# Last layer of a conditioned sequence model: where ScalarE's copies of matmul products stand in its order

## The reference

```python
h, gate = _adaln(x, c, adaln_mamba_w, adaln_mamba_b)
h_fwd = _ssm(h, fwd_in_w, fwd_xproj_w, ...)
h_bwd = jnp.flip(_ssm(jnp.flip(h, 1), bwd_in_w, ...), 1)
x = x + gate * (h_fwd + h_bwd)
h, gate = _adaln(x, c, adaln_mlp_w, adaln_mlp_b)
return x + gate * (jax.nn.silu(h @ mlp_w1) * (h @ mlp_w2) @ mlp_w3)

def _ssm(h, in_w, xproj_w, dt_bias, A_log, Dskip, out_w):
    xs, z = jnp.split(h @ in_w, 2, axis=-1)
    xs = jax.nn.silu(xs)
    proj = xs @ xproj_w                       # 512 dt, 64 B, 64 C
    dt = jax.nn.softplus(proj[..., :512] + dt_bias)
    # scan over tokens, 512 channels x 64 states:
    # hst = hst * exp(dt * A) + (dt * x) * B ;  y = sum over states of hst * C
    return (y + xs * Dskip) * jax.nn.silu(z) @ out_w
```

## Time and profile before

| | us |
|---|---|
| median of 3 runs (4523.04 to 4531.2) | 4526.49 |
| the profiled execution | 4523.65 |
| its span, first to last instruction | 4521.8 |

### The profile page before, as it was taken

How to read it: one execution, slowest core, us unless ns; L and a number is a source line. 1 busy time by engine, 2 the same in 40 slices (tenths; PEclk the granted TensorE clock), 3 DMA queues, 4 the chain that set the end, 5 groups by cost and what they waited for, 6 DMA issues and landing times.

```text
span 4521.8 us, 80784 instructions
## 1 busy us (share of the span) xinstructions
PE 4262.2 (94%) x31308; PEld 3470.6 (77%) x31308; DVE 4061.9 (90%) x3951; ACT 3941.5 (87%) x6178; POOL 3810.0 (84%) x1522
## 2 busy tenths in 40 slices
PE   8989899899899998999999999999999999999998
PEld 5448788778778774458888888888888888888887
DVE  5659999999899986649999999999999999999996
ACT  4559999899899974559999999999999999999995
POOL 3329999899889883339999999999998999999996
PEclk8999999999999999999999999999999999999999
DMA  4001221111111221022242322322322422323221
GB/s 165 1 15 68 57 64 64 56 59 64 57 57 65 63 82 40 1 45 71 73 86 75 91 65 79 80 74 80 82 76 69 83 80 90 64 80 64 76 81 39
DMA packets 241388, 303.31 MB, mean 67 GB/s; under 512 B 116448, under 2 KB 175712, under 8 KB 241008
## 3 DMA queue, kind: packets, MB, share of 16 engines
q1 hardware_dynamic: 241008, 298.15, 23.5%
HBM read 289.84 MB, written 8.26 MB: 66 GB/s over the span
## 4 chain that ended last, share of the span: by engine, by line
PE 41%; ACT 39%; DVE 12%; issue 5%; POOL 3%; DVEq 0%; DMA 0%; SPq 0%; POOLq 0%; ACTq 0%
PE psum L1109 11%; ACT weights_c L1684 10%; PE psum L1093 10%; PE psum L834 8%; ACT work L1705 8%; ACT work L1684 7%; ACT weights_c L1705 6%; DVE work L2155 6%; PE psum L1209 5%; DVE weights_c L2155 3%; PE psum L1090 2%; ACT L1416 2%; ACT modulation L1684 2%; POOL work L2573 1%; PE psum L1290 1%
## 5 line engine op out<-in xcount | busy, mean ns | idle before, releaser
L2573 POOL TENSOR_TENSOR work<-work,weights_a 128x2048 f32<-128x2048 f32 x512 | 1979.0, 3876 | 57.7 <-DVE work L2155 56.9
L2155 DVE TENSOR_TENSOR_SCAN work<-weights_c,psum 128x512 f32<-128x512 f32 x1316 | 1506.6, 1203 | 61.9 <-PE psum L1093 42.4
L1109 PE MATMUL psum<-ident,work 128*128 128x128 f32 x8192 | 1237.3, 274 | 12.1 <-POOL work L2573 11.8
L2573 POOL TENSOR_TENSOR weights_c<-weights_c,weights_a 128x2048 f32<-128x2048 f32 x256 | 990.4, 3877 | 14.2 <-DVE weights_c L2155 13.0
L1093 PE MATMUL psum<-ident,work 128*128 128x128 f32 x5464 | 952.5, 277 | 45.4 <-DVE weights_c L2155 13.3
L1109 PEld LDWEIGHTS psum<-ident,work 128*128 128x128 f32 x8192 | 968.0, 142 | 18.7 <-POOL work L2573 18.1
L1684 ACT ACTIVATE work<-work,decay 128x504 f32<-128x504 f32 x1172 | 819.0, 709 | 44.5 <-DVE weights_c L2155 24.1
L1093 PEld LDWEIGHTS psum<-ident,work 128*128 128x128 f32 x5464 | 658.9, 142 | 237.2 <-issue 129.3
L1093 PE MATMUL psum<-ident,weights_c 128*128 128x128 f32 x4432 | 784.9, 278 | 50.2 <-DVE work L2155 30.3
L2155 DVE TENSOR_TENSOR_SCAN work<-work,psum 128x512 f32<-128x512 f32 x586 | 675.9, 1202 | 24.0 <-PE psum L1093 17.0
L2155 DVE TENSOR_TENSOR_SCAN weights_c<-work,psum 128x512 f32<-128x512 f32 x586 | 677.5, 1203 | 20.9 <-PE psum L1093 18.5
(11 more groups left out here) (221 smaller groups left out, 6216.7 us busy)
## 6 DMA issues: line engine op xcount, KB each, us to landing
weights_a<-c_rows SPq DMA_DIRECT2D x384, 512.0 KB, 3.7
work<-b_diagonals SPq DMA_DIRECT2D x240, 128.0 KB, 2.4
weights_c<-b_diagonals SPq DMA_DIRECT2D x112, 128.0 KB, 2.4
b_diagonals<-weights_c SPq DMA_DIRECT2D x1, 4096.0 KB, 19.5
weights_c<-in_L_cond_fwd_in_w SPq DMA_DIRECT2D x8, 512.0 KB, 5.3
weights_c<-in_L_cond_fwd_xproj_w SPq DMA_DIRECT2D x4, 1024.0 KB, 7.1
weights_c<-in_L_cond_bwd_in_w SPq DMA_DIRECT2D x8, 512.0 KB, 5.2
weights_c<-in_L_cond_bwd_xproj_w SPq DMA_DIRECT2D x4, 1024.0 KB, 7.0
```

The lines of the kernel that those rows point to most:

```text
L1109: last = nc.tensor.matmul(PS[:, i, k * P:(k + 1) * P], flat[:, at:at + P], IDENT[:, :], start=begins and k == 0, stop=ends and k == DC - 1 ...
L2155: v.tensor_tensor_scan(buf["ring"][s % RING][:, along, j], buf["decay"][q % DECAYS[l]][:, along], PS[:, 4 + q % LOOKAHEAD, along], 0.0, AL ...
L2573: g.tensor_tensor(state, state, row.unsqueeze(2).broadcast_to([P, T, DC]), ALU.mult).then_inc(ss["prod_ready"], 1)
```

## The change

Five numbers in ScalarE's generator change, all of them the `later` of a copy in the last layer. For z the outer wait goes from 1 to 0 and the inner one from 2 to 0, for in and gate the inner one from 2 to 0: these copies stand two steps sooner, right behind ScalarE's own work of the step in which TensorE has the last piece. bt, dtx0 and dtx1 stand two steps sooner as well, and bc four steps sooner, two steps ahead of the one with its last piece. The copies of dt, the silu and softplus blocks, layer 1 and what is prepared before run 0 keep their places. Nothing is added or taken away, and the rows of TensorE, VectorE, GpSimd and SyncE are the same.

```diff
@@ scaled_inputs, of both state space layers
-                        yield plan.read(f"dtx{t}", 0 if l == 1 and r % 2 else 2)
+                        yield plan.read(f"dtx{t}", 0 if l == 3 or r % 2 else 2)
@@ beside3, of the last layer
                     def copy(name, dst):
-                        yield plan.read(name, 2)
+                        yield plan.read(name, 0)
...
                     def gates(*chunks):
                         for j in chunks:
-                            yield plan.read(f"z{j}", 1)
+                            yield plan.read(f"z{j}", 0)
...
-                        yield plan.read("bc", 2)
+                        yield plan.read("bc", -2)
...
-                        yield plan.read("bt", 2)
+                        yield plan.read("bt", 0)
```

## The result

| | us |
|---|---|
| median before, the 8 executions taken beside the changed kernel | 4526.9 (4522.63 to 4531.24) |
| median after, 8 executions | 4539.73 (4534.73 to 4541.15) |
| ratio, with its 95% interval | 1.0026 (1.0017 to 1.0035) |
| span of the profiled execution, before and after | 4521.8, 4537.0 |

What follows compares the result with a forecast made beforehand. No engine alone bounds the kernel; VectorE's scan chain is closest, with 82 us idle. Cost 11.2 us behind the silu blocks less 6.7 gained gave +4.5, 4531 us; forecast 4526 to 4535.5 (chance 0.60), range 4520 to 4542.

Steps and rivals of the forecast that it cites:

- What bounds the kernel: Last layer: no engine alone; VectorE's chained scans are closest, and an edit changes the time through VectorE's 82 us idle.
- The delay of the block: Silu blocks begin later because ScalarE waits for the copy right ahead: 1.0 us in run 0, 1.6 to 1.9 after.
- Passed on in full: Behind each silu block TensorE is already idle, so its waits grow by the whole delay and VectorE loses it: 11.2 us.
- The lower end: Behind the silu blocks, half the cost, 5.6 us, if TensorE uses its longer wait to work off what it was behind.
- the cost behind the blocks: Loss from later silu blocks in all stretches but run 7: 11.2 us, from 5.6 to 12.6.
- I cost it at nothing: Mid-run copies (z, in0 to in2, gate0 to gate2): ScalarE's waits, at most 1.8 us each, cost 0 us.
- three banks of reserve: Run 7's short silu block: 1.4 us more delay, which VectorE's three banks should swallow; otherwise the cost is 12.6 us.
- The gains: TensorE's waits for bank 7 go: bc 3.1 us, bt and dtx0 2.1, z0 1.5; together 6.7, lower end 3.0.
- The sum: Whole kernel: cost 11.2 less gains 6.7 us gives +4.5 us, 4531.0 on the median; from -1 to +9.6.
- rival 1: Banks free sooner, but something else holds TensorE there, so the full 11.2 to 12.6 us stay: 4535.5 to 4543, chance 0.20.
- Rivals 2 and 3: 2: later silu block is hidden, 4520 to 4526, chance 0.12. 3: prompt copies pay everywhere, 4517 or less, chance 0.08.
- rival 4: The change does nothing, cost and gains cancelling; it lies inside the forecast and has no chance of its own.

Runs made afterwards that it cites:

- run 0: Not a follow-up: the first of the last layer's stretches in every kernel; its silu block came 1.19 us later in the changed kernel.
- the table of transposes: TensorE transposes the identity in its waits behind the silu blocks: kernel before 4516.8 us, kernel before with ScalarE's self copies 4522.26, changed kernel 4524.95.
- three profiles of either kind: Blocks as before: kernel before, silu table loaded twice (4526.28 us), only bc, bt, dtx sooner (4522.33). Blocks late: changed kernel, only z, in, gate (4543.57), only last copies (4539.38).
- run 7: Not a follow-up: the last of the last layer's stretches in every kernel, with a short silu block; VectorE's idle time there was 0.0 us before, 0.9 after.
- the two halves: Kernel before with only bc, bt and dtx sooner, 4522.33 us (0.9993); and with only z, in and gate sooner, 4543.57 us (1.0036).
- The two self copies: Kernel before with ScalarE copying a finished chunk onto itself ahead of each silu block, once in run 0, twice in the others up to the sixth: 4536.08 us (1.0020).
- two equal table loads: Kernel before with the silu table loaded once more ahead of each silu block except that of run 7: 4526.28 us (0.9999).

## Why the prediction was right or wrong

- **What bounds the kernel** held: the loss is idle time of VectorE, 12.9 us of it between the two profiles, at the places that the text named and at two more.
- **The delay of the block**, by the arithmetic from product end to table load, came out in every run: predicted 1.0, then 1.6 to 1.9 us, measured 1.19, 1.94, 1.81, 1.72, 1.83, 1.73 and 1.71, 11.9 in all where 11.2 stood. In run 0 that is luck: nothing waited there, and the 1.19 us is z0's gain coming back. In runs 1 to 6 the end of the product sets the time as the arithmetic has it, but ScalarE waits only 0.15 to 0.61 us for the last copy, since the copies before it have already made it late.
- **"Passed on in full"** was right, and the table of transposes shows it to 0.1 us. The lower end, that TensorE works off half of it, has nothing for it.
- **The term that was mis-sized** is the cost behind the blocks, +11.2 us: it is 13.4 in the mean of three profiles of either kind, 11.9 for the delay and 1.5, which these runs do not tell from nothing, for TensorE's clock, and 16.7 in the two profiles compared. The prediction did not mention the clock at all, though in the kernel before it stood at 0.50 for 6 us behind the block of run 2, and took the 1.86 us of the earlier trace rows for a consequence of the wait alone.
- **"I cost it at nothing"** is the step that failed, for the mid-run copies. "A ScalarE that is late already waits less" is true: ScalarE's idle time ahead of L1584 is 22.7 us in 33 pieces, where I had expected 40 to 65 in 50. What does not follow is that the lag costs nothing. In runs 1 to 6 the mid-run lag alone delayed the silu blocks by 7.7 us, and it stays to whatever place comes next at which ScalarE is waited for: 1.7 us at steps 96 to 111 and 0.9 in run 7, which three banks of reserve did not swallow.
- **The gains** of bc, bt and dtx were right (5.8 us of idle time, 5.2 predicted), and the places are those predicted. z0's 1.0 us was there at its place and is no gain of its own, since ScalarE is full up to the next block.
- **The sum** with what was measured in place of each term: 11.9 + 1.5 for delay and clock, 1.7 + 0.9 for the lag, less 6.8, is +9.2 us. The medians say +12.8, with an interval from 7.7 to 15.8, so the sum is enough for it; whether 3 us more are hidden somewhere, these runs can't tell. Of the 4.7 us between +4.5 and +9.2 the lag has 2.6, the clock 1.5 and the delay 0.7.
- **The rivals.** The measured time lies where rival 1 had it, and for another reason: the gains arrived, the cost was larger. That it fell within the range at all is therefore luck: the part of the range above 4535.5 stood there for rival 1. Rivals 2 and 3 fell with the waits behind the blocks; rival 4 fell with the two halves, -4.5 and +16.7 us.

The rule against which the sum was weighed, "evacuate promptly" of the Trainium skill ("PSUM — Partial Sum Buffer", Summary: rules for kernel authors), holds here for bc, bt and dtx, at which another engine waited for the bank, and costs 16.7 us for the other copies, at all but one of which (z0 of run 0) none did.

## What to carry to other kernels

Move a copy out of PSUM ahead only where the trace shows someone waiting for the bank; anywhere else the engine that copies stands still for a product that isn't ready, and, if it has no gaps, carries that lag to the next place at which it is waited for. Follow such a lag to its first customer before costing it at nothing. The same holds for a gain: at z0 someone waited, but ScalarE had no gap up to the next block, and the gain came back there as a loss. Where TensorE stands idle and is needed at once afterwards, read the granted clock of the stretch behind the wait: transposes without a purpose in seven waits of 2.3 to 4.3 us were worth 11 us here, more than any of the moved copies.

## What the runs showed of the hardware

- **TensorE's clock behind a wait.** Behind waits of 3.1 to 6.1 us the granted clock fell to half in every profile of the kernels without transposes, for 3 to 7 us at a time. Behind the waits of 2.3 to 2.5 us (runs 1, 3 and 5 of the three profiles with the blocks as before) it fell in six places and stayed at 1.00 in three, with the same program and the same wait on both sides. With transposes in the wait it was at 1.00 behind every block, and four additions (L1109) took 0.60 us where they take 1.06 at half clock. The Trainium skill ("TensorE: Matmul & The Clock Gate", Why this matters for your kernels) warns of idle gaps between bursts of matmuls, which agrees with these rows.
- **A wait for one's own copy is cheap.** The two self copies, each waiting for the one before, took 1.30 us from the start of the first to the table load, 0.65 each. A copy of this size out of PSUM that waits for nothing takes 0.48 us of ScalarE's time (3100.43 to the next start at 3100.91), a decay or a scaled input 0.61; so the wait costs 0.17 us at most.
- **Of two equal table loads one is left.** The second load of the same table left no row in the trace (113 table loads with and without it) and no time. Whether it was dropped on the chip or before the program reached it, no run tells.
